# Score tiles of two shapes in a six-layer local attention: queries 0 to 63 as one 64x64 tile beside two 64x32 tiles

## The chip, the cores and the metric

The kernel runs on one core of one Trainium2 chip. Its time is device microseconds of one execution, and the median of several runs counts. TensorE (PE) multiplies and writes PSUM, VectorE (DVE), ScalarE (ACT) and GpSimd (POOL) compute element by element, and SyncE (SP) issues the transfers. All run side by side and meet at semaphores.

## The reference, cut to what matters

```python
x = x + xattn(layernorm(x), ctx, ...)            # once, 16 batches of 128x128
y = layernorm(x)
for i in range(6):
    y = attn_layer(shift_tokens(y), Wqkv[i], q_scale[i], k_scale[i], Wo[i]) + y
    y = ffn_layer(shift_tokens(y), ...) + y
return x + y
# inside attn_layer: 16 heads of 64, l2norm and rotary on q and k, then in windows of 32
bk2, bv2 = (look(bk), look(bv))                  # a window's keys and the window before it: 64 keys
mask = (it < jb) | (it > jb + w) | (jb == -1)
sim = einsum('bhwie,bhwje->bhwij', bq, bk2) * 8.0
attn = softmax(where(mask, -max, sim), -1)
out = einsum('bhwij,bhwje->bhwie', attn, bv2)
```

A query of window 0 may look at keys 0 to 31, one of window 1 at keys 0 to 63, one of window 2 at keys 32 to 95, one of window 3 at keys 64 to 127, each with the band mask inside.

## The kernel before, in words

One batch item in one layer is a unit: 6 x 16 = 96 units. Each engine runs its own fixed program: `step(s)` is called for s from -7 to 101 on every engine, and does for several units one stage each, since unit u is projected in step u, has its q and k transposed and its scores made in step u+1, its probabilities transposed in step u+2 and its values weighed in step u+3. Nothing is scheduled at run time. The order of the lines in `step` is the order of an engine's queue, and semaphores do the rest. Every fourth step also carries the feed-forward layer of four units (a quad), and between layers the weights are split into an upper and a lower part.

PE's step ends with `scores(s-1)`, and the next begins (after two feed-forward pieces in a quad's step) with `weigh_values`. In `scores` two bf16 matmuls of 128x512 (L406) first lay the band mask into the two PSUM banks S_BANK. Then 64 small matmuls (L412) add q times k: for each of eight head pairs c, for each of four windows g of 32 queries, for the even and the odd head (`odd`). The even head lies in SBUF partitions 0 to 63, the odd one in 64 to 127, so the two use different rows of the array. The stationary operand is q, 64 rows by 32 queries, the moving one is k, 64 keys. The output goes to PSUM partitions 32g to 32g+31. WINDOW_START gives the first key: 0, 0, 32, 64, so windows 0 and 1 already see the same 64 keys. An fp32 matmul leaves two records in the trace, each with its own weight load, so a unit has 128 of them.

The last head pair's eight matmuls each raise `s_ps`. On DVE `row_max` (L966) waits for all eight, and ACT's `exps` (L650) wait for `row_max`. `weigh_values` (L442) multiplies values and transposed probabilities in 64x64 tiles, four tiles side by side, with 64 or 32 moving columns. L389 to L391 are the projections (128x128 stationary, 512 moving), L396 and L423 are transposes, L452 is the output projection, L343 and L344 are the value projection of the cross attention with its bias as a one-row matmul.

Of the kernel before, what the change touches and what calls it, by code (L numbers as in the profile page):

```python
# [11 lines left out]
P = 128  # L12
# [4 lines left out]
E = 64  # L17
WIN = 32
# [23 lines left out]
SPAN = 64  # L42
WINDOW_START = [0, 0, 32, 64]
# [29 lines left out]
def build(nc, x_d, ctx_d, xw_d, xv_d, bv_d, wqkv_d, qk_scale_d, wo_d, w1_d, w2_d, vec_d, rope_d, const_d, out_d):  # L73
    def sb(name, shape, dt=F32):
        return nc.alloc_sbuf_tensor(name, shape, dt)
# [34 lines left out]
    kT = sb("kT", [P, 2, 8, P])  # L110
# [40 lines left out]
    def sem(name):  # L151
        return nc.alloc_semaphore(name)

    def sems(name, n):
# [15 lines left out]
    ss_clamped, ln_done, rn_guess, rn_ready, s_ps, max_ready, o_ps = (  # L170
        sem(s) for s in ("ss_clamped", "ln_done", "rn_guess", "rn_ready", "s_ps", "max_ready", "o_ps"))
# [43 lines left out]
    def par(u):  # L215
        return u % 2
# [8 lines left out]
    with block as block:  # L225
# [96 lines left out]
        def _(pe):  # L322
# [76 lines left out]
            def scores(u):  # L399


                for c in range(4):
                    if c == K0:
                        pe.wait_ge(tq_ready[c], u + 1)
                for odd in range(2):
                    mm(ps[:, S_BANK[odd], :], ident16[:], band16[:].rearrange("p c w -> p (c w)"), start=True, stop=False,  # L406
                       skip_group_check=True)
                for c in range(BLOCKS):
                    for g in range(P // WIN):
                        for odd in range(2):  # L410
                            r, q = slice(E * odd, E * odd + E), slice(WIN * g, WIN * g + WIN)
                            i = mm(ps[q, S_BANK[odd], c * SPAN:(c + 1) * SPAN], qT[r, par(u), c, q],  # L412
                                   kT[r, par(u), c, WINDOW_START[g]:WINDOW_START[g] + SPAN],
                                   start=False, stop=c == BLOCKS - 1, skip_group_check=True)
                            if c == BLOCKS - 1:
                                i.then_inc(s_ps, 1)
# [69 lines left out]
            def step(s):  # L486
# [70 lines left out]
                if live(s, 1):  # L557
                    scores(s - 1)
# [284 lines left out]
        def _(dve):  # L843
# [118 lines left out]
                              ps[:, TQ_BANK[c], :]).then_inc(tq_ready[c], 1)  # L962

            def row_max(u):
                dve.wait_ge(s_ps, 8 * u + 8)
                V.tensor_reduce(nmax[:].rearrange("p o c -> p (o c)"),  # L966
                                ps[:, S_BANK[0]:S_BANK[1] + 1, :].rearrange("p o (c w) -> p (o c) w", c=BLOCKS), AX.X, ALU.max,
                                negate=True).then_inc(max_ready, 1)
# [63 lines left out]
            def step(s):  # L1032
                run_quad(s, 7, ffn_stats)
                run_quad(s, 8, ffn_affine)
                run(s, 3, copy_o, 0)
                run(s, 2, inverse_sum, 0)
                run(s, 1, lower_w, V0)
                run(s, 0, rotary, Q0)
                run(s, 0, lower_w, Q0)
                run(s, 0, rotary, Q1)  # L1040
                run(s, 0, lower_w, Q1)
                run(s, 0, sum_squares, Q1)
                run_quad(s, 8, ffn_lower)
                run_quad(s, 9, ffn_gated, 2)
                run(s, 2, inverse_sum, 1)
                run(s, 3, add_residual)
                run(s, 0, sum_squares, Q0)
                run(s, 0, rotary, K1)
                run_quad(s, 9, ffn_residual)
                run(s, 0, sum_squares, K1)  # L1050
                run(s, 0, rotary, K0)
                run_input(s, 9, lower_xt)
                run(s, 0, sum_squares, K0)
                run(s, 0, clamp_norm)
                run(s, 1, row_max)
                run_quad(s, 8, ffn_gated, 0)
                run_quad(s, 7, ffn_normalise)
                run_quad(s, 8, ffn_gated, 1)
                run(s, 0, copy_v, 1)
                run(s, 0, copy_v, 0)  # L1060
                run_layer(s, -8, rope_tables, 1)
# [68 lines left out]
```

## Time and profile before

| | us |
|---|---|
| runs | 1728.39, 1739.47, 1734.22; median 1734.22 |
| the profiled execution | 1738.27, its span 1736.5 |
| PE busy | 1532.5 (88% of the span) |
| DVE busy | 1360.1 (78%) |
| POOL busy | 1264.0 (73%) |
| ACT busy | 1244.8 (72%) |

Busy is the time in which an engine has at least one instruction in flight. A small matmul's record lasts some 0.2 us although the next on another tile starts a few ns later, so for PE the distance from start to start says what a matmul costs, and the length of a record says little.

### The profile page before, as it was taken

The numbers are of one execution on the slowest core, as the hardware profiler recorded it, in microseconds if no ns is written. First come the engines' busy times: TensorE is split into PE (matmuls) and PEld (weight loads), VectorE is DVE, ScalarE is ACT, GpSimd is POOL, SyncE is SP. The second block draws the span as 40 slices with busy tenths as digits, with TensorE's granted clock in tenths as the row PEclk, the third lists the DMA queues.
The fourth block names the chain that finished last, engine by engine and source line by source line (L and its number), as shares of the span: only waits on it lengthen the run. The fifth ranks groups of instructions, "written<-read, shape, count | busy, mean of one in ns | idle before, by whom it ended". The sixth has DMA issues, their size and how long they took to land.

```text
span 1736.5 us, 67874 instructions
## 1 busy us (share of the span) xinstructions
PE 1532.5 (88%) x28560; PEld 1223.3 (70%) x28656; DVE 1360.1 (78%) x2564; ACT 1244.8 (72%) x4601; POOL 1264.0 (73%) x1492
## 2 busy tenths in 40 slices
PE   6589989899998899999889998989999989989985
PEld 5367777677777677777667777767777767777774
DVE  4678888878887977877878787787788787887873
ACT  3267868777877777777777777786776777776773
POOL 2378787777877867867767768787778687887770
PEclk8699999999999999999999999999999999999998
DMA  4012211021211111211111212111211112111011
GB/s 120 1 40 57 57 40 52 27 58 33 67 57 35 45 47 45 67 45 47 33 28 57 67 38 60 33 40 46 57 51 47 47 33 57 27 49 45 27 45 31
DMA packets 50878, 80.62 MB, mean 46 GB/s; under 512 B 8947, under 2 KB 16806, under 8 KB 50574
## 3 DMA queue, kind: packets, MB, share of 16 engines
q1 hardware_dynamic: 50574, 76.28, 15.8%
q8 instruction: 226, 3.70, 0.9%
q14 instruction: 78, 0.64, 0.1%
HBM read 18.62 MB, written 1.05 MB: 11 GB/s over the span
## 4 chain that ended last, share of the span: by engine, by line
PE 63%; ACT 12%; DVE 11%; issue 7%; POOL 7%; DMA 0%; SPq 0%; POOLq 0%; DVEq 0%
PE ps L442 9%; PE ps L389 7%; PE ps L396 7%; ACT pr L650 7%; PE ps L412 6%; PE ps L452 6%; PE ps L391 5%; PE ps L390 5%; PE ps L423 4%; PE ps L483 4%; DVE v L956 2%; ACT sq L613 2%; PE ps L406 2%; POOL t L779 2%; POOL t L798 2%
## 5 line engine op out<-in xcount | busy, mean ns | idle before, releaser
L779 POOL TENSOR_TENSOR t<-t 128x512 f32<-128x512 f32 x384 | 486.2, 1279 | 84.2 <-DVE t L951 83.6
L650 ACT ACTIVATE pr<-ps,nmax 128x64 f32<-128x64 f32 x1536 | 460.6, 353 | 0.9 <-DVE nmax L966 0.9
L798 POOL TENSOR_TENSOR t<-t,rn 128x512 f32<-128x512 f32 x384 | 397.6, 1056 | 7.5
L650 ACT ACTIVATION_READ_ACCUMULATOR pr<-ps,nmax 128x1 f32 x1536 | 376.8, 248 | 0.0
L949 DVE TENSOR_TENSOR t<-ps,rope 128x512 f32<-128x512 f32 x384 | 261.6, 681 | 58.1 <-PE ps L396 37.9
L809 POOL TENSOR_TENSOR pr<-pr,rsum 128x512 f32<-128x512 f32 x192 | 200.8, 1046 | 135.1 <-DVE rsum L973 134.4
L389 PE MATMUL ps<-w_hi,xt_hi 128*128 128x512 f32 x576 | 272.7, 473 | 26.7 <-DVE t L951 10.3
L613 ACT ACTIVATE sq<-ps 128x512 f32<-128x512 f32 x384 | 233.3, 622 | 69.9 <-PE ps L391 63.2
L951 DVE TENSOR_TENSOR t<-ps,rope 128x512 f32<-128x512 f32 x384 | 260.7, 679 | 0.0
L931 DVE TENSOR_REDUCE ss<-sq 128x8 f32<-128x512 f32 x384 | 259.2, 675 | 0.7
L390 PE MATMUL ps<-w_lo,xt_hi 128*128 128x512 f32 x576 | 235.0, 408 | 3.0 <-issue 3.0
L391 PE MATMUL ps<-w_hi,xt_lo 128*128 128x512 f32 x576 | 235.7, 409 | 0.7 <-issue 0.7
L396 PE MATMUL ps<-consts,t 128*128 128x128 f32 x1536 | 220.9, 276 | 14.4 <-ACT qT L641 11.2
L956 DVE COPY v<-ps 128x512 f32<-128x512 f32 x192 | 131.8, 690 | 123.4 <-PE ps L391 122.7
L396 PEld LDWEIGHTS ps<-consts,t 128*128 128x128 f32 x1536 | 177.2, 141 | 62.5 <-ACT qT L641 41.6
L442 PE MATMUL ps<-pT,v_win 64*64 64x32 f32 (+1 forms) x6144 | 167.9, 218 | 48.2 <-issue 47.9
L452 PE MATMUL ps<-wo,oT 128*128 128x128 f32 x1536 | 190.0, 277 | 3.9 <-DVE oT L983 3.8
L442 PE MATMUL ps<-pT,v 64*64 64x64 f32 (+1 forms) x3072 | 166.7, 228 | 25.2 <-issue 22.1
L389 PEld LDWEIGHTS ps<-w_hi,xt_hi 128*128 128x128 f32 x576 | 112.2, 195 | 108.6 <-DVE v L956 52.4
L442 PEld LDWEIGHTS ps<-pT,v_win 64*64 64x64 f32 x6144 | 150.5, 135 | 52.9 <-issue 52.8
L452 PEld LDWEIGHTS ps<-wo,oT 128*128 128x128 f32 x1536 | 179.0, 192 | 9.0 <-DVE oT L983 8.7
L442 PEld LDWEIGHTS ps<-pT,v 64*64 64x64 f32 x3072 | 139.4, 135 | 43.9 <-issue 39.2
(122 smaller groups left out, 2714.0 us busy)
## 6 DMA issues: line engine op xcount, KB each, us to landing
v_win<-v SPq DMA_DIRECT2D x384, 128.0 KB, 2.3
wqkv<-wqkv_in SPq DMA_DIRECT2D x36, 256.0 KB, 3.9
xsh<-xr SPq DMA_DIRECT2D x24, 224.0 KB, 2.6
wo<-wo_in SPq DMA_DIRECT2D x6, 512.0 KB, 3.8
w<-w_in SPq DMA_DIRECT2D x6, 342.0 KB, 4.6
w<-w_in SPq DMA_DIRECT2D x6, 172.5 KB
x<-x_in SPq DMA_DIRECT2D x4, 256.0 KB, 4.1
out<-x SPq DMA_DIRECT2D x4, 256.0 KB, 2.7
```

Source lines behind the costliest of these rows:

```text
L389: mm(o, xt_hi[:, xslot(u), :], w_hi[:, w], start=True, stop=False)
L390: mm(o, xt_hi[:, xslot(u), :], w_lo[:, w], start=False, stop=False)
L391: mm(o, xt_lo[:, xslot(u), :], w_hi[:, w], start=False, stop=True).then_inc(qkv_ps[c], 1)
L396: i = tr(ps[:, TQ_BANK[c], k * P:(k + 1) * P], t1[:, c, k * P:(k + 1) * P], ident)
L442: i = mm(ps[E * b:E * b + E, O_BANK[odd], j * P + q:j * P + q + m], window[:, c * E:(c + 1) * E], pT[E * odd:E * odd + E, c, q:q + m], sta ...
L452: i = mm(ps[:, Y_BANK, 0:P], oT[:, par(u), c, :], wo[:, c, :], start=c == 0, stop=c == 7)
L613: A(sq[:, c, :], ps[:, QKV_BANK[c], :], ACT.Square).then_inc(sq_ready[c], 1)
L650: i = A(pr[:, c, odd * SPAN:(odd + 1) * SPAN], ps[:, S_BANK[odd], c * SPAN:(c + 1) * SPAN], ACT.Exp, bias=nmax[:, odd, c:c + 1], accum_out ...
L779: G.tensor_tensor(t1[:, c, :], t1[:, c, :], t2[:, c, :], ALU.add).then_inc(qk_added[c], 1)
L798: G.tensor_tensor(w, w, rn[:, par(u), h2, a, :].unsqueeze(2).broadcast_to([P, 8, E]), ALU.mult).then_inc(done, 1)
L949: V.tensor_tensor(t1[:, c, :].rearrange("p (h e) -> p h e", h=8), bank.rearrange("p (h e) -> p h e", h=8), cos, ALU.mult)
L951: V.tensor_tensor(t2[:, c, :].rearrange("p (h a e) -> p h a e", h=8, a=2), bank.rearrange("p (h a e) -> p h a e", h=8, a=2)[:, :, ::-1, :] ...
```

## The change

For each head pair and half, the queries 0 to 63 (windows 0 and 1, whose keys are the same 64) become one matmul with a 64x64 stationary tile. Windows 2 and 3 stay 64x32 tiles. The count of matmuls in a unit falls from 64 to 48, that of the semaphore's raises from 8 to 6. Nothing else is touched, and the result in PSUM has the same layout.

```diff
+                pieces = [(0, 2 * WIN, 0), (2 * WIN, WIN, WINDOW_START[2]), (3 * WIN, WIN, WINDOW_START[3])]
                 for c in range(BLOCKS):
-                    for g in range(P // WIN):
+                    for t, n, first in pieces:
                         for odd in range(2):
-                            r, q = slice(E * odd, E * odd + E), slice(WIN * g, WIN * g + WIN)
+                            r, q = slice(E * odd, E * odd + E), slice(t, t + n)
                             i = mm(ps[q, S_BANK[odd], c * SPAN:(c + 1) * SPAN], qT[r, par(u), c, q],
-                                   kT[r, par(u), c, WINDOW_START[g]:WINDOW_START[g] + SPAN],
+                                   kT[r, par(u), c, first:first + SPAN],
                                    start=False, stop=c == BLOCKS - 1, skip_group_check=True)
...
             def row_max(u):
-                dve.wait_ge(s_ps, 8 * u + 8)
+                dve.wait_ge(s_ps, 6 * u + 6)
```

On PE, the place between the mask matmuls and the next projections, in the step of the first unit. The two numbers after the names are columns of the stationary operand and moving columns, and x64 is the count of such matmuls in a row.

```order
 L383 MATMUL ps<-consts,xr 128x128 x4
 L406 MATMUL ps<-band,ident 128x512 x2
-L412 MATMUL ps<-kT,qT 32x64 x64
+L413 MATMUL ps<-kT,qT 64x64 x2
+L413 MATMUL ps<-kT,qT 32x64 x4
+L413 MATMUL ps<-kT,qT 64x64 x2
...
 L389 MATMUL ps<-w_hi,xt_hi 128x512
 L390 MATMUL ps<-w_lo,xt_hi 128x512
```

The pair of rows (64x64 x2, then 32x64 x4) stands there eight times, once for each head pair. What was one run of 64 matmuls of one shape is now sixteen short runs of two shapes in turn. On ACT, POOL, DVE and SP the order is the same as before.

## Rows read from the trace of the kernel before

**Rows 1.** Page, part 1: busy us, share of the span, instructions of each engine.
```profile
PE 1532.5 (88%) x28560; PEld 1223.3 (70%) x28656; DVE 1360.1 (78%) x2564; ACT 1244.8 (72%) x4601; POOL 1264.0 (73%) x1492
```
**Rows 2.** Page, part 4: the chain that ended last, by engine.
```profile
PE 63%; ACT 12%; DVE 11%; issue 7%; POOL 7%; DMA 0%; SPq 0%; POOLq 0%; DVEq 0%
```
**Rows 3.** Busy time by stretch, the layers; columns: busy us of each engine, granted clock.
```profile
core 0: us, PE busy (x) PEld busy (x) DVE busy (x) ACT busy (x) POOL busy (x), PEclk, DMA share, GB/s
100.00:1705.00 1605.00, 1454.88 (x28019) 1165.63 (x28113) 1294.57 (x2387) 1204.84 (x4514) 1225.30 (x1437) 0.98 0.17 46
```
**Rows 4.** Groups of PE by shape: busy us, mean ns, idle before.
```profile
L412 PE MATMUL ps<-kT,qT 64*32 64x64 f32 x12288 | 146.9, 226 | 11.8 <-issue 11.8
```
**Rows 5.** Timeline of PE, one unit: start us, length us, count [idle before].
```profile
844.46 0.38 PE L406 MATMUL ps<-band,ident 128*128 128x512 bf16 x1
844.77 1.49 PE L412 MATMUL ps<-kT,qT 64*32 64x64 f32 x128
846.19 0.27 PE L442 MATMUL ps<-pT,v 64*64 64x64 f32 x1
...
846.29 0.22 PE L442 MATMUL ps<-pT,v 64*64 64x64 f32 x1
```
**Rows 6.** The same block in two narrow windows, up to 844.83 and up to 844.90.
```profile
844.77 0.29 PE L412 MATMUL ps<-kT,qT 64*32 64x64 f32 x8
...
844.77 0.34 PE L412 MATMUL ps<-kT,qT 64*32 64x64 f32 x15
```
**Rows 7.** Line L412: duration ns, smallest, median, largest.
```profile
L412 PE MATMUL ps<-kT,qT x12288: 212/216/311, 97.2 to 1690.6; 64*32 64x64 f32 x199
```
**Rows 8.** Timeline of PE, a unit with a pause in its last head pair.
```profile
780.33 0.32 PE L412 MATMUL ps<-kT,qT 64*32 64x64 f32 x8 [0.67 <-issue]
780.57 0.27 PE L442 MATMUL ps<-pT,v 64*64 64x64 f32 x1
```
**Rows 9.** Timeline of PE, from the weighing of values to projections.
```profile
849.26 0.22 PE L442 MATMUL ps<-pT,v 64*64 64x32 f32 x1
849.41 0.50 PE L389 MATMUL ps<-w_hi,xt_hi 128*128 128x512 f32 x1
849.75 0.40 PE L390 MATMUL ps<-w_lo,xt_hi 128*128 128x512 f32 x1
849.98 0.40 PE L391 MATMUL ps<-w_hi,xt_lo 128*128 128x512 f32 x1
850.22 0.40 PE L389 MATMUL ps<-w_hi,xt_hi 128*128 128x512 f32 x1
```
**Rows 10.** Timeline of PE: cross attention, two shapes in turn; below one shape alone.
```profile
17.00 0.48 PE L343 MATMUL ps<-xw,ctxT 128*120 128x128 f32 x2
17.41 0.47 PE L344 MATMUL ps<-bv,ones 1*120 1x128 f32 x2
17.82 0.48 PE L343 MATMUL ps<-xw,ctxT 128*120 128x128 f32 x2
...
871.52 1.95 PE L452 MATMUL ps<-wo,oT 128*128 128x128 f32 x16
```
**Rows 11.** Who waited for whom, PE alone: us in total, times, longest.
```profile
PE ps L442 <- issue: 69.9, 58, 2.3
PE ps L423 <- POOL pr L809: 15.3, 12, 2.4
PE ps L412 <- issue: 11.8, 18, 1.5
...
PE ps L396 <- ACT qT L641: 11.2, 27, 0.9
```
**Rows 12.** Timeline of PE: a pause inside the weighing of values.
```profile
848.89 0.27 PE L442 MATMUL ps<-pT,v 64*64 64x32 f32 x2 [1.46 <-issue]
```
**Rows 13.** A stretch ahead of a fall of the clock (columns of Rows 3).
```profile
876.00:880.00 4.00, 1.95 (x12) 1.43 (x11) 4.00 (x10) 1.90 (x5) 4.00 (x4) 0.92 0.01 4
```
**Rows 14.** Timeline of PE at the lower clock: projections, start to start.
```profile
87.21 0.63 PE L390 MATMUL ps<-w_lo,xt_hi 128*128 128x512 f32 x1
87.64 0.63 PE L391 MATMUL ps<-w_hi,xt_lo 128*128 128x512 f32 x1
```
**Rows 15.** Line L966 on DVE, duration; and what waits for the scores.
```profile
L966 DVE TENSOR_REDUCE nmax<-ps x96: 1209/1223/1227, 101.1 to 1691.0; 128x16 f32<-128x1024 f32 x96
...
  PE ps L412: 19.2, 17
```
**Rows 16.** The chain of waits, ACT at its exps: start us, us, what.
```profile
803.15 0.49 ACT qT L641
803.63 2.36 ACT pr L650 x16
```

## The prediction

> **What bounds the kernel now.** I read the page first. PE is busy for 88% of the span, the next engine for 78% [rows 1], and the chain that ended last lies on PE for 63% [rows 2]. In the layers, from 100 to 1705 us, PE is busy for 1454.88 of 1605 us and its granted clock is 0.98 of full speed, so nearly all at 2.4 GHz [rows 3]. PE is the bound, with 1605 - 1454.88 = 150 us without a record in flight. Hence a microsecond added to PE's work costs between nothing and a microsecond: nothing as long as it fills a part of these 150 us.
>
> The scores look cheap. Their 12288 records keep PE busy for 146.9 us [rows 4], 1.5 us in each of 96 units. In the timeline one block of 128 records starts at 844.77 and lasts 1.49 us [rows 5]. The last record itself lasts 0.22 us [rows 7], so from the first start to the last start it is 1.27 us, or 9.9 ns a record. That is far under the length of a record: eight tiles work side by side.
>
> Next I looked at where PE goes from one shape of tile to another. The last L412 started at 844.77 + 1.49 - 0.22 = 846.04, and the first L442, a 64x64 tile with 64 moving columns, at 846.19 [rows 5]: 0.15 us, where records inside the block follow at 0.01. The first four L442 start together, and their second passes come 0.10 after the first [rows 5]. The block of L412 itself begins with eight records in 0.05 us (length 0.29 with the last one's 0.24), and the 15th ends at 0.34, so it started at 0.12 and the ninth at about 0.08 [rows 6].
>
> **Is that 0.15 a price of the shape?** Three places say so. In a unit with a pause the last eight records of the scores, by the code's order the two passes of windows 2 and 3 of the last head pair, run from 780.33, and the last starts at 780.33 + 0.32 - 0.22 = 780.43. The tiles over PSUM partitions 0 to 63 had been through before the pause of 0.67 us. The next matmul, into partitions 0 to 63, still starts only at 780.57, 0.14 later [rows 8]. So it is not its own corner of the array that it waits for. From 64x64 tiles to 128x128 ones the step is again 0.15 (849.26 to 849.41), with only 32 moving columns in front of it, and the next record comes 0.34 later where it is 0.23 afterwards [rows 9]. In the cross attention 128 rows and 1 row alternate every two records: a round of four takes 17.82 - 17.00 = 0.82 us, where records of such size in one shape follow at (1.95 - 0.28) / 15 = 0.11, four in 0.44 [rows 10]. Two changes of shape cost 0.38 us there, 0.19 each.
>
> Seen from the rows, each change of shape empties the array, and then the first weight loads stand in the open. The Trainium skill has this as a rule (TensorEngine Tiling (Array Packing), Key Properties): changing the tiling mode, and not just the tile, drains TensorE. The trace agrees with its 0.15 us. By that rule all 16 boundaries of the new block pay, which gives the 250 us below; the page names no time, and without the rule the sum would be that of the first rival.
>
> **The change, part by part.**
> Removed: 16 of 64 matmuls in a unit, 32 of 128 records. If only the count mattered, 32 x 9.9 ns = 0.32 us in a unit would go, 30 us in 96.
> Added: the 64x64 tiles. One head pair is now two such tiles with two passes each, then four 64x32 tiles with two passes each. Nothing in the trace has this mixture, so I build it from its two halves. The first half: passes 0.10 apart as in the first L442s, the odd head's 0.01 behind: 0.11 from first to last start [rows 5]. To the next shape 0.15, as from L412 to L442, also after 64 moving columns. The second half: second pass at 0.08, three more tiles at 0.007: 0.10 [rows 6]. Back again 0.15; this direction (32 columns to 64) is the very one that rows 5 and 8 show. Together 0.11 + 0.15 + 0.10 + 0.15 = 0.51, with unrounded starts 0.50. Eight head pairs: 4.0 us up to the next block's first matmul, where it is 1.27 + 0.15 = 1.42 now. That is 2.6 us more in a unit, and 2.6 x 96 = 250 us in all. The bounds of one boundary: from 0.01 (no price) to the 0.19 of 128-wide tiles on top of their pass.
>
> What of it lies beside other work? PE's idle time. The largest part is inside or at the edge of the small tiles: L442 69.9 us and L412 11.8 us, released by nothing that the profile shows [rows 11], such as 1.46 us in the midst of one run of L442 [rows 12]. These pauses follow the densest stretches, 128 records in 1.27 us and then 96 more. The new block has 96 records in 4.0 us, so whatever supplies the instructions has three times as long. I take 70 of these 82 us as gone. The other waits are for engines with a quarter of their time free: L423 on POOL 15.3, L396 on ACT 11.2 and smaller ones [rows 11], together the rest of 150, about 68. They gain slack in every unit, but part of this is the plain way from an engine back to PE; I take 20 as gone. So 90 us of the 250 vanish in waits, 160 stay. I add 5 for more time at the lower clock.
>
> What is late next: `row_max` takes 1.22 us and waits for the scores; the wait is seldom now, 19.2 us in 17 of 96 units [rows 15], and will be the rule. Behind it on DVE stand the copies of V, which PE's next projections into those banks need. PE meanwhile weighs values (1.1 us undisturbed) and projects V for 0.7, so the first copy is asked for after `row_max` is done: no charge. On ACT eight exps of a half take 2.36 us and a copy 0.49 [rows 16]; both start later by what the block grew, as PE's own following work does, so this loop stretches with PE and not beyond it. The two semaphore raises saved and the fewer waits of DVE on them: nothing, since DVE waits for the last one anyway.
>
> The sum: 1738.27 + 250 - 90 + 5 = 1903 against the profiled execution, which lies 4 us above the median of the runs, so 1900.
>
> **The rivals.**
> 1. No price between the shapes here (the change gains). The 64x64 tile covers one half of the array's columns and the two 64x32 tiles the other, in each half of the rows; no row above shows two shapes that don't overlap with each other in a loop. If they then run side by side, it goes by the count: 1734 - 30 = 1704, if a record keeps its 9.9 ns. If instead the 64x64 tile sets the pace with a pass each 0.10 (16 passes, 1.6 us, against 1.27), it is 1734 + 32 = 1766; at 0.08 nothing changes. Against it speaks the unit with the pause, where an idle corner of the array did not help [rows 8]. The point from which it decides is the boundary's price: below some 0.02 us on 16 boundaries the saved 0.32 us outweigh it. 8 in 100: 5 for a gain, 2 for no change, 1 for a small loss.
> 2. Nothing is absorbed: the pauses in L442 stay since they come from elsewhere, and the added 2.6 us go fully onto the span: 1734 + 250 = 1984. For it: the chain is on PE for 63% only and other loops also contain the scores. Against it: the pauses' place. 9 in 100.
> 3. The clock. It fell after a stretch with PE busy for 1.95 of 4 us [rows 13]. In the new block moving columns stream in perhaps half of the time. At the lower level of 1.2 GHz a projection takes 0.43 us from start to start [rows 14] in place of 0.23 [rows 9]. If 3 us in each unit ran so, 3 x (1 - 0.23/0.43) = 1.4 us would be lost, 134 in all: 1900 + 134 = 2034. Against it: the records stay in flight almost without a gap. 8 in 100.
>
> **How the numbers follow.** The forecast has 75 in 100. Its own ends: all of the 150 us filled but a rest of 15, 1734 + 250 - 135 = 1849; or 20 us absorbed and the boundary at its rows' price, 1964. The range goes to 1990 to take in rival 2 and the milder cases of rival 3, and starts at 1850; outside are rival 1, most of rival 3 and little else. Faster by over 1%, about what this kernel's measurement can tell from no change: 0.05. Within 1%: 0.03. Slower: 0.92.
>
> **What would show it.** In the trace after, a unit's block of scores should be about 4 us from its first start to the start of the next block, in 16 runs, with 0.14 to 0.15 us at each change of shape, 96 records instead of 128. L413's busy time should go from 147 us to above 350. PE's pauses "issue" before L442 should fall from 70 to about 10 us, PE's busy share should rise above 92%, and the other engines' shares fall by a tenth with their busy us unchanged. DVE's wait for the scores should rise beyond 100 us. The forecast is wrong if the block takes 1.0 to 1.6 us (rival 1), if the idle time of PE stays at 150 us (rival 2), or if the granted clock in the layers falls under 0.93 (rival 3).

## The result

The changed kernel takes 1869.82 us (median of four runs; 1867.55 to 1871.01) against 1736.85 us of the kernel before (also four). The ratio is 1.0772, with a 95% interval of 1.0734 to 1.0809: slower by 7.7%, 133 us. The forecast was 1900 with a range of 1850 to 1990. The direction and the mechanism were right, the size was 30 us too large.

### The profile page after: what moved, and what is told of

It reads as the page before. It is cut to its first block, busy times and chain, and to the rows that moved or that the text cites. A ratio compares the mean times of both kernels' runs of the same rounds, so it can differ in the third digit from the quotient of the medians.

```text
span 1868.0 us, 61826 instructions
## 1 busy us (share of the span) xinstructions
PE 1750.2 (94%) x25584; PEld 1333.5 (71%) x25584; DVE 1371.5 (73%) x2564; ACT 1244.2 (67%) x4601; POOL 1262.5 (68%) x1492
## 4 chain that ended last, share of the span: by engine, by line
PE 66%; ACT 15%; DVE 12%; POOL 5%; issue 1%; DMA 0%; SPq 0%; POOLq 0%; DVEq 0%
PE ps L413 20%; ACT pr L651 9%; PE ps L443 6%; PE ps L396 5%; PE ps L389 5%; PE ps L424 5%; PE ps L453 4%; PE ps L484 4%; PE ps L391 3%; PE ps L390 3%; DVE xh L1001 3%; ACT sq L614 2%; ACT qT L642 2%; PE ps L406 2%; DVE v L957 2%
## 5 line engine op out<-in xcount | busy, mean ns | idle before, releaser
L413 PE MATMUL ps<-kT,qT 64*32 64x64 f32 (+1 forms) x9216 | 396.5, 233 | 0.0
L651 ACT ACTIVATION_READ_ACCUMULATOR pr<-ps,nmax 128x1 f32 x1536 | 381.7, 253 | 0.0
L413 PEld LDWEIGHTS ps<-kT,qT 64*32 64x32 f32 (+1 forms) x9216 | 268.0, 113 | 153.7 <-issue 40.7
L389 PE MATMUL ps<-w_hi,xt_hi 128*128 128x512 f32 x576 | 265.9, 462 | 26.9 <-DVE t L952 13.4
L967 DVE TENSOR_REDUCE nmax<-ps 128x16 f32<-128x1024 f32 x96 | 117.6, 1225 | 205.6 <-PE ps L413 205.6
L391 PE MATMUL ps<-w_hi,xt_lo 128*128 128x512 f32 x576 | 229.4, 398 | 0.0
L390 PE MATMUL ps<-w_lo,xt_hi 128*128 128x512 f32 x576 | 228.4, 397 | 0.0
L661 ACT ACTIVATE oT<-ps 128x512 f32<-128x512 f32 x96 | 57.0, 593 | 204.2 <-PE ps L443 204.2
L389 PEld LDWEIGHTS ps<-w_hi,xt_hi 128*128 128x128 f32 x576 | 108.8, 189 | 110.8 <-DVE v L957 54.1
```

Of the source, the lines that this page charges most:

```text
L389: mm(o, xt_hi[:, xslot(u), :], w_hi[:, w], start=True, stop=False)
L390: mm(o, xt_hi[:, xslot(u), :], w_lo[:, w], start=False, stop=False)
L391: mm(o, xt_lo[:, xslot(u), :], w_hi[:, w], start=False, stop=True).then_inc(qkv_ps[c], 1)
L651: i = A(pr[:, c, odd * SPAN:(odd + 1) * SPAN], ps[:, S_BANK[odd], c * SPAN:(c + 1) * SPAN], ACT.Exp, bias=nmax[:, odd, c:c + 1], accum_out ...
```

## The profile after

The page of the changed kernel, its part 1 (busy us, share, instructions; compare [rows 1]) and the first line of its part 4, the chain that ended last [rows 2]:

```profile
PE 1750.2 (94%) x25584; PEld 1333.5 (71%) x25584; DVE 1371.5 (73%) x2564; ACT 1244.2 (67%) x4601; POOL 1262.5 (68%) x1492
...
PE 66%; ACT 15%; DVE 12%; POOL 5%; issue 1%; DMA 0%; SPq 0%; POOLq 0%; DVEq 0%
```

PE has a tenth fewer instructions and is in use for 218 us more. The other engines do what they did before in a longer span. "Issue", 7% of the chain before, is down to 1%. The layers in one stretch (columns as in [rows 3]):

```profile
100.00:1840.00 1740.00, 1674.53 (x25174) 1279.11 (x25174) 1304.02 (x2384) 1204.89 (x4514) 1223.00 (x1433) 1.00 0.15 42
```

PE has 65 us without a record in flight, where it had 150, and the granted clock is 1.00, where it was 0.98.

One unit of the changed kernel in the timeline of PE, cut at 983.0 in the first two rows and begun at 985.7 in the others (start us, length us, count):

```profile
981.26 0.59 PE L406 MATMUL ps<-band,ident 128*128 128x512 bf16 x2
981.78 1.35 PE L413 MATMUL ps<-kT,qT 64*64 64x64 f32 x28
...
985.60 0.32 PE L413 MATMUL ps<-kT,qT 64*32 64x64 f32 x8
985.84 0.27 PE L443 MATMUL ps<-pT,v 64*64 64x64 f32 x1
```

The block runs from 981.78 to 985.84, 4.06 us to the next matmul's start; before it was 1.42 [rows 5]. The cut shows the pace: 28 records reach to 983.13, less 0.23 for the last one's own length that is 1.12 from first to last start, two rounds of twelve records (0.51 each) and the first four of a third (0.11). The last start of the block is at 985.60 + 0.32 - 0.22 = 985.70 and L443 follows 0.14 later, as in [rows 5]. Taken from the records one by one, a head pair is: 64x64 tiles at 0 and 7 ns, their second passes at 107 and 114, then 64x32 tiles at 262, 269, 275, 282, their second passes at 342 to 362, and the next head pair at 508. The prediction had 0.50.

Who waited for whom in the changed kernel (us in total, times, longest us), first in all, then PE alone:

```profile
POOL pr L810 <- DVE rsum L974: 222.2, 139, 13.4
DVE nmax L967 <- PE ps L413: 205.6, 96, 7.5
ACT oT L661 <- PE ps L443: 204.2, 73, 3.7
...
PEld ps L389 <- DVE v L957: 54.1, 166, 0.9
...
PE ps L459 <- DVE xh L1001: 24.6, 19, 7.6
PE ps L389 <- DVE t L952: 13.4, 14, 2.7
...
PE ps L396 <- ACT qT L642: 10.1, 29, 0.8
PE ps L424 <- POOL pr L810: 7.9, 11, 0.8
```

Of the pauses that headed PE's list before [rows 11], those of the weighing and of the scores, 0.9 us is left, in one place ahead of the weighing; the other engines now wait for PE's scores and for what follows them, DVE in 96 of 96 units [rows 15].

**Where the time went.** The profile's "idle before" starts when the last record in flight has ended, some 0.2 us after the last start, so it shows a pause too short. I therefore took every interval from one matmul's start to the next and gave it to the earlier one's line:

| us, start to start | before | after | difference |
|---|---|---|---|
| scores (L412, L413) | 158.7 | 389.8 | +231.0 |
| weighing of values (L442, L443) | 233.9 | 148.1 | -85.8 |
| projections (L389 to L391) | 531.8 | 520.5 | -11.3 |
| all else | | | -2.3 |
| span | 1736.5 | 1868.0 | +131.5 |

The block of scores itself is steady. From first to last start it takes 1.268 us (within 0.02) in 75 of the 96 units before, and 21 are longer, by 16.3 us together. After, it takes 3.914 in practically all. The weighing takes 1.382 us where it runs undisturbed. Before, its 96 blocks were 85.8 us longer than that in all, 64 of them by more than 0.1; after, 0.1 us in all. So the change adds 96 x (3.914 - 1.268) = 254 us, and 16.3 + 85.8 = 102 us of pauses disappear. (A few us of these 102 aren't pauses in the strict sense: four of the blocks ran partly at the lower clock, and some intervals were only a little long.)

## Experiments

Two theories stood against each other on the 254 us. **D**: each change of tile shape costs about 0.14 us, whatever the shapes do otherwise. **W**: the 64x64 fp32 tile is slow by itself, its weight load being twice as wide. And two on the 102 us. **S**: PE runs out of instructions after dense stretches. **P**: the pauses belong to the small tiles' work.

### e1: the two shapes in two groups

```diff
-                for c in range(BLOCKS):
-                    for t, n, first in pieces:
+                for c, (t, n, first) in [(c, x) for part in (pieces[:1], pieces[1:]) for c in range(BLOCKS) for x in part]:
```

> The changed kernel with its 48 score matmuls in another order: first the sixteen 64x64 ones of all head pairs, then the thirty-two 64x32 ones. Same tiles, same count, one boundary between the shapes instead of fifteen. Theory D (each change of shape costs about 0.15 us from start to start, wherever it stands): the block from its first start to the next matmul is 16 passes of the 64x64 tiles at 0.06 to 0.10 us, 0.15, 16 passes of the 64x32 tiles at 0.06 to 0.08, 0.15, so 2.2 to 3.2 us in place of 4.06, and the time is 1755 (1740 to 1800). Theory W (the fp32 64x64 tile itself, with its 64-column weight load, is the slow thing, and the order does not matter): the block stays near 4 us and the time near 1870.

Measured: 1700.74 us, 0.9764 of the kernel before (0.9733 to 0.9794), so faster than both. The block in the timeline of PE:

```profile
847.52 2.18 PE L413 MATMUL ps<-kT,qT 64*64 64x64 f32 x96
849.62 0.27 PE L443 MATMUL ps<-pT,v 64*64 64x64 f32 x1
```

The same 96 records of the same tiles take 2.10 us up to the next matmul instead of 4.06. W falls. Inside a group a 64x64 tile's passes follow each other at 0.058 us, the 64x32 tiles' at 0.056, so a 64-column weight load costs next to nothing more there than a 32-column one. That is the quick end of the bracket for the passes. It puts the block just under D's 2.2 to 3.2 us and the time 54 us under its 1755, outside its 1740 to 1800: the price of a boundary stands, the passes were put too slow. The block is 0.69 us longer than in the kernel before (66 us in all), and yet the kernel is faster by 41: 26 us of pauses are left where there were 102. The projections take 15.6 us less from start to start, and PE, which rests less, spends 68 us at the lower clock in place of 115; how much each of these is worth was not tried by itself.

### e2: two head pairs taken together

```diff
-                for c in range(BLOCKS):
-                    for t, n, first in pieces:
+                for c, (t, n, first) in [(c, x) for k in range(0, BLOCKS, 2) for part in (pieces[:1], pieces[1:])
+                                         for c in (k, k + 1) for x in part]:
```

> The changed kernel with the score matmuls of two head pairs taken together: their four 64x64 ones, then their eight 64x32 ones. Seven boundaries between the shapes inside the block instead of fifteen. Theory D: each boundary gone saves 0.15 us less the distance of two passes in one tile (0.06 to 0.09), so the block falls from 4.06 to about 3.3 us, and the time to about 1815. Theory W: no change, 1870. If the price depended on how full the array is before the boundary, the saving would be smaller than half of that of the grouped version.

Measured: 1800.67 us, 1.0336 of the kernel before (1.0299 to 1.0374). Its block takes 2.798 us from first to last start, 2.94 to the next matmul, less than the 3.3 expected since the passes are quick here too. In the timeline (3.01 less the last record's 0.22):

```profile
94.32 3.01 PE L414 MATMUL ps<-kT,qT 64*64 64x64 f32 x96
```

With 16, 8 and 2 runs of one shape the same 96 records take 3.914, 2.798 and 1.960 us. Each boundary less saves (3.914 - 2.798) / 8 = 0.1395 us and (2.798 - 1.960) / 6 = 0.1397 us. Both steps remove as many boundaries of one direction as of the other, so this is the mean of the two directions. It is a fixed price, neither more after a long run nor less after a short one.

### e3: 64x64 tiles only

The scores of window 3 are left out.

```diff
-                pieces = [(0, 2 * WIN, 0), (2 * WIN, WIN, WINDOW_START[2]), (3 * WIN, WIN, WINDOW_START[3])]
+                pieces = [(0, 2 * WIN, 0), (2 * WIN, 2 * WIN, WINDOW_START[2])]
...
-                dve.wait_ge(s_ps, 6 * u + 6)
+                dve.wait_ge(s_ps, 4 * u + 4)
```

> The changed kernel with windows 2 and 3 made as one 64x64 tile as well, with the keys of window 2 for both; the scores of window 3 are therefore left out (64 records in a unit, all of one shape, and the same shape as the weighing of values that follows). Theory D: no boundary inside and none towards the weighing, so the block takes 16 passes at 0.06 to 0.10, 1.0 to 1.6 us up to the next matmul, and the time is 1690 to 1735, since the pauses in the dense part become fewer. Theory W: 64x64 tiles are slow by themselves, the block stays above 2.5 us and the time above 1800.

Measured: 1635.76 us, 0.9394 (0.9364 to 0.9424). Both the time and the block are better than D's ranges (1690 to 1735 us, 1.0 to 1.6 us), the block only just:

```profile
113.23 1.16 PE L413 MATMUL ps<-kT,qT 64*64 64x64 f32 x64
114.21 0.22 PE L443 MATMUL ps<-pT,v 64*64 64x64 f32 x1
```

From 113.23 to 114.21 it takes 0.98 us. The last score starts at 113.23 + 1.16 - 0.22 = 114.17 and L443 0.04 later: from 64x64 to 64x64 nothing is charged, though banks, tensors and the semaphore change. Four 64x64 tiles, each with sixteen passes at 0.058, are as quick as the two of e1's first group, so those two leave room for two more.

### e4: fewer matmuls of the old shape

The kernel before with the scores of window 1 left out.

```diff
-                    for g in range(P // WIN):
+                    for g in (0, 2, 3):
...
-                dve.wait_ge(s_ps, 8 * u + 8)
+                dve.wait_ge(s_ps, 6 * u + 6)
```

> The kernel before with the scores of window 1 left out: 48 matmuls of 64x32 and nothing else, 96 records in a unit. This is the gain by count alone that the first rival of the prediction promised. If the block is paced by the issue of records (9.9 ns each), it takes 0.95 us instead of 1.27, and the time falls by about 30 us, a little more if the pauses become fewer: 1690 to 1705. If it is paced by the passes inside a tile (16 of them at 0.06 to 0.08 us), the block stays at 1.2 to 1.3 us and the time at 1725 to 1736.

Measured: 1668.79 us, 0.9578 (0.9547 to 0.9609), below both ranges. In the timeline (1.19 less the last record's 0.22):

```profile
95.15 1.19 PE L412 MATMUL ps<-kT,qT 64*32 64x64 f32 x96
```

The block goes from 1.268 to 0.977 us, 10.2 ns a record. This total alone doesn't separate the two readings: sixteen passes at the 0.056 to 0.058 us that e1 showed would come out at 0.90 to 0.93. The single starts do. From the second to the fifth, the rounds of six records follow at 0.056 us, the pace of the passes. From the 25th record on it is 10.3 ns a record, and in the kernel before, from the 33rd on, 10.5, so nearly the same with six tiles as with eight. There the count of records sets the pace, as the first rival had it. That is 28 us of the 73. The pauses brought more, from 102 to 54 us: removing a quarter of the records from the densest stretch halves them.

### e5: the values weighed later

The kernel before, in which six records of projections stand between the two dense blocks in three steps of four.

```diff
-    v = sb("v", [P, 2, 2, 512])
+    v = sb("v", [P, 3, 2, 512])
...
-                if live(s, 3):
+                if live(s, 3) and due(s, 9):
                     bank_free(s, (x_updated, 4))
...
                     weigh_values(s - 3)
...
                     project(s - 1, V0)
+                if live(s, 3) and not due(s, 9):
+                    bank_free(s, (x_updated, 4))
+                    bank_free_of_input(s, 10)
+                    bank_free_of_quad(s, x_final, 10, 1, NQ)
+                    weigh_values(s - 3)
...
-                run(s, 2, copy_o, 1)
                 run(s, 1, exps, 0)
                 run(s, 0, upper_w, V1)
                 run(s, 1, exps, 1)
+                run(s, 2, copy_o, 1)
```

> The kernel before (64 score matmuls of 64x32) with the weighing of values taken out from behind the scores: in the three steps of four without feed-forward pieces between them it now comes after the two projections of V (0.7 us each, only six records). For that V gets three buffers instead of two, and ACT's copy of the weighed values comes after its exps instead of before. Theory S (the 102 us of pauses inside the small-tile blocks of the kernel before are PE running out of instructions: each pause ends 2.2 to 2.9 us after the start of a 16 KB transfer on the instruction queue): 1.4 us with six records between two dense blocks let the fetch catch up, the pauses fall from 102 to under 50 us and the time from 1737 to 1650 to 1690. Theory P (the pauses belong to the small tiles themselves, through PSUM or the array): they stay near 100 us, and the time moves by less than 15 us.

Measured: 1675.50 us, 0.9658 (0.9641 to 0.9675). PE's list of waits has 9.9 us before L442 where it had 69.9 [rows 11]:

```profile
PE ps L412 <- issue: 18.4, 26, 1.3
...
PE ps L442 <- issue: 9.9, 23, 1.4
```

Start to start the pauses are 47 us in place of 102, 26 of them now in the scores. The two blocks are as dense as before and their work is the same, so P falls and S stands. Not all of the 61 us are pauses, though: the projections are 15 us shorter from start to start (516.9 against 531.8), and their weight loads are held back by DVE's copies of V for 20 us in place of 52.

### e6: grouped, and the values weighed later

e1 with the edits of e5.

> The same move on top of the grouped version of the changed kernel (e1, 1701 us). Its pauses are only 26 us. Theory S: they go to nearly nothing, and the projections no longer wait for DVE's copies of V (54 us of weight loads held back in the changed kernel, mostly beside other work): 1665 to 1690. If e5 gains and this one does not, the gain of e5 was the pauses; if both gain alike, it was the order of the copies.

Measured: 1673.74 us, 0.9639 (0.9615 to 0.9662). The pauses are 1.6 us in all, and the page shows PE busy at 93% of a shorter span:

```profile
PE 1547.5 (93%) x25488; PEld 1257.0 (75%) x25584; DVE 1352.5 (81%) x2564; ACT 1247.0 (75%) x4601; POOL 1263.5 (76%) x1492
```

It gains 27 us over e1 by the medians (33 between the profiled executions, 22 by the two ratios, since the two ran on different occasions) where e5 gained 61 over the kernel before. From start to start the weighing is 19 us shorter than in e1 and the projections about 15, as in e5. So the answer lies between the two that were put up: the same 15 us come in the projections in both, and what e5 gains beyond e6 is pauses. e5 and e6 lie within each other's spread: e5 keeps the shorter block and 47 us of pauses, e6 has the block of 1.960 us and none.

### e7: a rest between the blocks

The kernel before with one more wait.

```diff
                     bank_free_of_quad(s, x_final, 10, 1, NQ)
+                    if live(s, 2):
+                        pe.wait_ge(max_ready, s - 1)
                     weigh_values(s - 3)
```

> The kernel before with one wait more and nothing else: before it weighs values, PE waits until DVE's row maximum of the scores just made is there, 1.2 us after the end of the scores. 96 x 1.2 = 115 us of rest for PE in all, in about a quarter of the steps hidden behind feed-forward pieces: 86 us. Theory S: the instructions keep coming during the rest, so the pauses inside the weighing go from 86 to under 15 us, and the time rises by only 0 to 30 us. Theory P: the pauses stay as they are and the time rises by 60 to 90 us, to about 1815.

Measured: 1872.85 us, 1.0783 (1.0755 to 1.0810). As a time this is near neither theory, because the rest came out almost twice as long as I had put it. DVE is often not free when the scores are done (`row_max` starts 0.26 us after the last score at the earliest, 0.80 in the median), so the wait from the last score to the first weighing grew from 25.7 us in all to 176.9, 151 us more instead of 86:

```profile
PE ps L442 <- DVE nmax L968: 100.6, 50, 2.9
PE ps L442 <- issue: 57.9, 31, 2.7
...
PE ps L389 <- DVE t L953: 11.5, 11, 2.8
```

The "issue" of this list is mostly that wait as well, at the first L442 of a unit. Inside the weighing, the intervals of more than 0.24 us fell from 80.7 to 9.0 us, which is S's forecast for the pauses; inside the scores, which have no rest before them, they stayed (15.7 us before, 16.9 here). And the clock, which fell more often with such rests, took much of the gain away again. In the layers:

```profile
100.00:1840.00 1740.00, 1515.59 (x28020) 1222.87 (x28113) 1285.16 (x2387) 1213.62 (x4515) 1227.27 (x1437) 0.94 0.15 42
```

0.94 here against 0.98 before [rows 3]; L389 and L390 alone took 27 us more than in the kernel before, and 44 of the 96 weighing blocks ran at least partly at the lower clock. A slower PE also uses up its instructions more slowly, but the 52 blocks at full clock have 4.7 us of such intervals between them, where the 93 of the kernel before had 74. The run supports S in the trace and missed in its sum.

### e8: only the side edits of e5

e5 with `weigh_values` back in its place; V's third buffer and ACT's order stay.

> The version e5 with its main edit undone: the values are weighed right behind the scores as in the kernel before, while V keeps its three buffers and ACT's copy of the weighed values stays behind its exps. It says how much of e5's 61 us the two side edits brought. If the pauses of PE's instructions were all of it, this is the kernel before again, 1730 to 1740 with about 100 us of pauses. If ACT's order mattered, it is lower, down to 1700, with the pauses unchanged.

Measured: 1743.81 us, 1.0016 (0.9990 to 1.0043), with 109 us of pauses. The side edits by themselves bring nothing; e5's gain comes with the place of the weighing.

### e9: the 64x32 group first

```diff
-                for c, (t, n, first) in [(c, x) for part in (pieces[:1], pieces[1:]) for c in range(BLOCKS) for x in part]:
+                for c, (t, n, first) in [(c, x) for part in (pieces[1:], pieces[:1]) for c in range(BLOCKS) for x in part]:
```

> The grouped version e1 with its two groups exchanged: the thirty-two 64x32 matmuls first, the sixteen 64x64 ones after them. In three of four steps the block is then followed by the weighing of values, which is 64x64 too. Theory D: towards the weighing there is no change of shape any more, so the first L443 starts 0.04 to 0.06 us after the last score matmul instead of 0.146, and the second passes there come after 0.06 to 0.08 instead of 0.107. That is 0.10 to 0.14 us in 72 steps, 7 to 10 us: 1691 to 1694. If the price hangs on the change of program stage (other banks, a semaphore) and not on the shape, it stays 0.146 and the time 1701.

Measured: 1691.06 us, 0.9715 (0.9685 to 0.9746). In the timeline the weighing begins while the last scores are still to come:

```profile
114.91 0.27 PE L443 MATMUL ps<-pT,v 64*64 64x64 f32 x1
114.92 0.27 PE L443 MATMUL ps<-pT,v_win 64*64 64x64 f32 x1
114.96 0.23 PE L413 MATMUL ps<-kT,qT 64*64 64x64 f32 x2
```

In 70 of the 72 units where the two blocks meet, the first L443 starts 0.05 us before the last score, where D had it 0.04 to 0.06 after and e1 has it 0.146 after. The second pass of the weighing, however, still comes 0.105 us after the first, not 0.06 to 0.08. From the first score to the last L443, where nothing pauses, it is 3.330 us in place of e1's 3.488: 0.158 less, about one boundary's price. Against e1 that is 10 us by the medians and 8.5 by the two ratios, since the two ran on different occasions; D gave 7 to 10 for 72 boundaries.

## Why the prediction was right, point by point

**The price of a boundary.** Right, in mechanism and in size. The step "together 0.51, with unrounded starts 0.50" measured 0.508, the block 4.06 where it said 4.0, and the whole 254 us where it said 250. It was built from two halves that the trace of before showed singly: the weighing's first two passes after a change of shape, and the scores' first two. e2 and e1 show that it is per boundary, e3 and e9 that it vanishes where the shape stays. The rule of the Trainium skill (TensorEngine Tiling (Array Packing), Key Properties) holds here, with 0.14 us for each drain; that page's other property, that different tiles can load weights and multiply in parallel, showed here only among tiles of one shape.

**The first rival**, that the two shapes would run side by side since they cover different parts of the array, is refuted by the changed kernel itself: between a 64x64 tile over output partitions 0 to 63 and a 64x32 one over 64 to 95 lie 0.148 us in every head pair. What it said on the count was right for one shape (e4: 28 us for 32 records, where it had 30).

**The waits that vanish.** Here lay the error of size. The prediction took 70 of 82 us of pauses and 20 us of the rest as gone, and added 5 for the clock: 165 net. The trace shows 102 us of pauses, all of them gone, and about 20 elsewhere (11.3 in the projections, 6.5 ahead of the first L442 of a unit, 2.3 in all else). The mis-sized term is the 82: it is the profile's "idle before", counted from the end of the last record in flight, while the lost time runs from the last start. And "an instruction supply that has three times as long" was not only better but sufficient. The sum with the measured terms is 254 - 102 - 20 = 132. Against the forecast's 1903 for the profiled execution, which took 1869.79, that is 4 us more for the block, 32 less for the pauses and 5 less for the clock.

**The second rival** (nothing absorbed) fell with it, by e5 and by the changed kernel's list of waits. **The third**, the clock, went the other way: with PE resting less, the granted clock in the layers rose to 1.00, and the time at the lower level fell from 115 to 63 us, of which 56 lie before and after the layers. The 5 us for it had the wrong sign. e7 shows that the fear was not empty: there PE rests 1.8 us on average between the scores and the weighing, and the time at the lower level is 280 us.

**What was to be seen**: L413 busy above 350 us (396.5), PE's share above 92% (94%), DVE waiting for the scores beyond 100 us (205.6), the copies of V without a charge (54.1 us of weight loads held back, 52.4 before by the same list) all came. "About 10 us" of pauses before L443 were 0.9, and the others' shares fell by 6 to 7%, not by a tenth.

**A row misread.** "Weighs values (1.1 us undisturbed)" is too short: that stretch held 76 of the unit's 96 records, and a block without a pause takes 1.38 us from first to last start. It changed nothing, since a longer weighing gives DVE's copy of V only more time.

**What the prediction did not see**: that the same tiles in another order gain. It priced the boundary and the count, found +250 and -30, and did not ask what is left with one boundary.

## What stays open

Each of the 77 pauses over 0.24 us in the small-tile blocks of the kernel before ends 2.1 to 2.9 us after the start of a transfer on the instruction queue, each pause after a transfer of its own, and the same holds for the 61 of e5, the 28 of e1 and the 40 of e4. A moment picked at random in the kernel before has such a transfer in one case of nine. The transfers themselves go with PE's work: for 57216 matmuls and weight loads there are 226, for the 51168 of the changed kernel 202, so 253 instructions for each in both, while the instructions of the other engines are the same. From part 3 of the two pages, before and after (transfers, MB, share):

```profile
q8 instruction: 226, 3.70, 0.9%
...
q8 instruction: 202, 3.31, 0.7%
```

One pause is that of 1.46 us in [rows 12]. The transfers from 844.5 to 849 us, in 40 slices, have one that starts at 846.2:

```profile
DMA  0000000000000006000000000000000000000000
...
q8 instruction: 1, 0.02, 1.6%
```

A transfer takes about 1 us and the pause ends some 1.4 us after that (medians over the 77). This, with e5, e7, e8 and the changed kernel, makes the supply of instructions the cause. What fills the 1.4 us, how much PE holds in reserve, and why the other 149 transfers of the kernel before go by without such a pause, no run here shows. Nor was a version tried that makes all scores with fewer than 128 records and in one shape.

## What to carry to other kernels

Small matmuls of different tile shapes belong in groups: a change of shape cost 0.14 us here, as much as fourteen records, and that turned a saving of a quarter of the score matmuls into a loss of 7.7%; once grouped by shape the same matmuls gave a gain of 2.4 to 2.9%. Where hundreds of tiny matmuls follow one another, look for pauses inside runs that wait for nothing, and try a few large matmuls between the dense blocks before cutting down the number of small ones. And measure such blocks from start to start, since the busy time of short records and the idle time between them both mislead.

## What the runs showed of the hardware

- A change of tile shape costs a fixed 0.14 us (0.1395 and 0.1397 by two differences), also between tiles over different SBUF and PSUM partitions. It is the mean of the two directions between 64x64 and 64x32.
- Inside one shape, a pass of an fp32 tile with 64 moving columns follows the one before it in the same tile after 0.056 us (64x32) or 0.058 us (64x64), as long as two to four tiles work side by side. With six it is 0.061 on average and with eight about 0.08, where the records' own 10 ns bind.
- PE lost 102 of 1736 us in pauses inside runs of small matmuls in the kernel before. In e4 a quarter fewer score records cut that by half, and 1.4 us of large matmuls after the scores removed three quarters of what lay in the weighing.
- A rest for PE of 1.8 us on average in each unit raised the time at the lower clock of 1.2 GHz from 115 to 280 us.
